# Expert layer of a graph network and feed-forward kernel: ten large and seven small steps in one slot space instead of thirteen and four, small ones placed between large ones, and the bias rows written one step later

## What is computed

```python
# x: (1250, 1024); _layernorm(x) is t
logits = silu(t @ rw1 + rb1) @ rw2 + rb2            # router, 8 experts
vals, idx = top_k(logits, 2)
w = softmax(masked to the two)                       # two weights per token
eh = silu(einsum('td,edh->teh', t, ew1) + eb1)       # 1024 -> 256, each expert
eo = einsum('teh,ehd->ted', eh, ew2) + eb2           # 256 -> 1024, each expert
y = t + einsum('te,ted->td', w, eo)
return x + y
```

## Time and profile before

| | us |
|---|---|
| median of 3 runs (1177.22 to 1178.97) | 1178.7 |
| the profiled execution, its own time | 1178.53 |
| its span, first to last instruction | 1176.7 |
| what lies around the span | 1.83 |
| first W1 matmul of step 0 | at 927.75 |
| first W1 matmul of step 1, of step 16 | at 943.29, at 1146.76 |

### The profile page before, as it was taken

One profiled execution on the slowest core, in us unless ns is written; L12 is line 12 of the kernel. 1 busy time (PEld: TensorE's weight loads), 2 busy tenths in 40 slices (PEclk: granted clock), 3 DMA queues, 4 the chain that ended last, 5 costly groups with the idle time before them and its releaser, 6 DMA issues.

```text
span 1176.7 us, 18108 instructions
## 1 busy us (share of the span) xinstructions
PE 1082.0 (92%) x6504; PEld 1025.6 (87%) x6504; DVE 630.8 (54%) x1115; ACT 446.1 (38%) x935; POOL 153.8 (13%) x171
## 2 busy tenths in 40 slices
PE   2699999999989999999999999999995599999984
PEld 1699999999989999999998999999994588898883
DVE  5738888888743353235333432642224467777762
ACT  5644444435311222121222021553332466666651
POOL 2000000000000001000100200014421223343311
PEclk9999999999999999999999999999997699999977
DMA  5402332123126560034003400765560779999973
GB/s 130 138 15 88 102 102 67 58 82 102 67 67 206 167 183 1 1 101 114 6 1 125 118 1 1 215 209 155 171 215 0 291 224 299 279 268 262 247 179 54
DMA packets 73658, 150.45 MB, mean 128 GB/s; under 512 B 12346, under 2 KB 51191, under 8 KB 69073
## 3 DMA queue, kind: packets, MB, share of 16 engines
q1 hardware_dynamic: 61117, 112.34, 30.8%
q0 software_dynamic: 11840, 36.22, 12.3%
q10 hardware_dynamic: 596, 0.48, 0.1%
HBM read 109.97 MB, written 44.53 MB: 131 GB/s over the span
## 4 chain that ended last, share of the span: by engine, by line
PE 76%; DVE 8%; DMA 5%; issue 5%; ACT 4%; DVEq 1%; ACTq 0%; POOL 0%; POOLq 0%; SPq 0%; PEld 0%
PE ps L1384 19%; PE ps L866 13%; PE ps L1456 9%; PE ps L1115 8%; PE ps L1423 7%; PE ps L2012 5%; DMA out<-o_rows,to_i 4%; PE ps L732 3%; PE ps L670 2%; PE ps L2028 2%; DVE w_lo L2094 2%; ACT w_hi L2048 1%; PE ps L654 1%; PE ps L1998 1%; DVE key_hot L725 1%
## 5 line engine op out<-in xcount | busy, mean ns | idle before, releaser
L739 DVE TENSOR_TENSOR adj<-ps,adj 125x250 f32 x212 | 87.8, 414 | 43.5 <-PE ps L732 35.4
L866 PE MATMUL ps<-h_lo,w_hi 128*128 128x418 f32 x336 | 108.5, 371 | 0.0
L1346 POOL TENSOR_TENSOR s_rows<-s_rows,b1t 125x1368 f32<-125x1368 f32 (+3 forms) x9 | 23.5, 2627 | 625.7 <-DMA s_rows<-in_x 625.7
L866 PE MATMUL ps<-h_hi,w_hi 128*128 128x418 f32 x336 | 100.3, 379 | 0.0
L1423 PE MATMUL ps<-z_hi,adj 125*125 125x342 f32 (+1 forms) x300 | 95.1, 322 | 1.6 <-DVE s_rows L1655 1.6
L1423 PE MATMUL ps<-z_lo,adj 125*125 125x342 f32 (+1 forms) x300 | 94.3, 319 | 1.9 <-issue 1.9
L866 PE MATMUL ps<-h_hi,w_lo 128*128 128x418 f32 x336 | 93.5, 359 | 0.0
L2012 PE MATMUL ps<-xt_hi,w_hi 128*128 128x256 f32 (+1 forms) x272 | 82.7, 304 | 10.1 <-DVE w_lo L2094 8.6
L1115 PE MATMUL ps<-adj,y_hi 125*128 125x416 f32 (+1 forms) x240 | 86.7, 361 | 3.4 <-issue 3.4
L2094 DVE TENSOR_TENSOR w_lo<-w_raw,w_hi 128x2048 fp32r<-128x2048 f32 x34 | 76.5, 2289 | 21.3 <-ACT w_hi L2048 19.9
L1115 PE MATMUL ps<-adj,y_lo 125*128 125x416 f32 (+1 forms) x240 | 86.2, 359 | 0.4 <-issue 0.4
(11 more groups left out here) (294 smaller groups left out, 2691.6 us busy)
## 6 DMA issues: line engine op xcount, KB each, us to landing
w_raw<-in_L_ffn_ew SPq DMA_DIRECT2D x34, 1024.0 KB
xin<-in_x SPq DMA_DIRECT2D x10, 448.0 KB
t_d<-xn SPq DMA_DIRECT2D x10, 448.0 KB
base<-x_d POOLq DMA_DIRECT2D x10, 448.0 KB, 4.1
out<-base POOLq DMA_DIRECT2D x10, 448.0 KB, 3.4
y_d<-y_hi SPq DMA_DIRECT2D x7, 625.0 KB
y_d<-y_lo SPq DMA_DIRECT2D x7, 625.0 KB
self_d<-self SPq DMA_DIRECT2D x7, 625.0 KB
```

The source lines that it names most:

```text
L739: e.tensor_tensor(cols, ps[0:P, 5 + b % 2, 0:KW].rearrange("p (t w) -> p t w", t=NT), cols, ALU.add).then_inc(self.took, 1)
L866: mm = e.matmul(BANK(m, own, c), wt[:, own, k, :], ht[:, k, a:a + w], start=(k == 0 and p == 0), stop=(k == KT - 1 and p == 2))
```

## The change

The table of slots gets 10 large and 7 small steps: still 17 steps, but 27 blocks (28 columns in the tables, which want an even count). Large steps own slots 0 to 2559 and small ones the 896 slots behind. A small remainder of an expert goes into a small step counted from the end, and into a large one from the end if the small ones are used up; the arithmetic for that replaces the old one by the same number of linked VectorE operations. A list `ORDER` says which step runs when. By size (L large, S small) the order of execution was L x13, S x4 and is now

`S L L S L S L L S L L S L S L L S`

On ScalarE `head(t)` now comes before `shift(t-1)`, and the wait for the slot weights and the bias rows moves from ahead of the first step into the first `shift`.

```diff
-BIG, SMALL = 13, 4
+BIG, SMALL = 10, 7
 NS = BIG + SMALL
-NBLK = BIG * SUB + SMALL
+BLOCKS_IN_USE = BIG * SUB + SMALL
+NBLK = BLOCKS_IN_USE + BLOCKS_IN_USE % 2
+ALL_SLOTS, BIG_SLOTS = 128 * BLOCKS_IN_USE, BIG * M
-BLOCKS = lambda s: SUB if s < BIG else 1
-BLOCK_AT = lambda s: min(SUB * s, BIG * (SUB - 1) + s)
+ORDER = (10, 0, 1, 11, 2, 12, 3, 4, 13, 5, 6, 14, 7, 15, 8, 9, 16)
+BLOCKS = lambda t: SUB if ORDER[t] < BIG else 1
+BLOCK_AT = lambda t: min(SUB * ORDER[t], BIG * (SUB - 1) + ORDER[t])
+BLOCKS_TO = lambda t: sum(BLOCKS(i) for i in range(t)) if t >= 0 else -SUB
...
-            link(e.tensor_scalar(at, at, first[:, 0, NX:NX + 1], None, ALU.add))
-            link(e.tensor_scalar(halved[:], at, 0.5, BIG * M / 2.0, ALU.mult, ALU.add))
-            link(e.tensor_tensor(jump[:], at, halved[:], ALU.min))
-            link(e.tensor_tensor(jump[:], jump[:], filled[:], ALU.subtract))
+            link(e.tensor_scalar(at, at, first[:, 1, NX:NX + 1], 2.0 * ALL_SLOTS, ALU.subtract, ALU.add))
+            link(e.tensor_scalar(halved[:], at, 0.5, None, ALU.mult))
+            link(e.scalar_tensor_tensor(out=at, in0=at, scalar=-float(BIG_SLOTS), in1=halved[:], op0=ALU.add, op1=ALU.min))
+            link(e.tensor_tensor(jump[:], at, filled[:], ALU.subtract))
             link(e.tensor_tensor(jump[:], jump[:], start, ALU.subtract))
...
                 for b in range(BLOCKS(s)):
                     for half in range(2):
-                        e.wait_ge(m_out, GROUP_AT(s - 1) + 2 * NB + 2 * b + half + 1)
+                        if s > 0:
+                            e.wait_ge(m_out, GROUP_AT(s - 1) + 2 * NB + min(2 * b + half + 1, 2 * BLOCKS(s - 1)))
...
             def shift(s, u, q):
-                x = e.value_load(step_x[0:1, ds(s, 1)], min_val=0, max_val=NX - 1)
+                x = e.value_load(step_x[0:1, ds(ORDER[s], 1)], min_val=0, max_val=NX - 1)
+                if s == 0:
+                    e.wait_ge(g_to, 2)
+                    e.wait_ge(g_b2, 16)
                 e.wait_ge(m_kept, s + 1)
...
             w1(0, 0, 0)
             rows(0, 0, 0)
-            e.wait_ge(g_to, 2)
-            e.wait_ge(g_b2, 16)
-            pipeline(e, NS, (1, shift), (0, head))
+            pipeline(e, NS, (0, head), (1, shift))
```

More of the change, by code:

```diff
@@ L63 @@
 SUB = M // 128
-BIG, SMALL = 13, 4
+BIG, SMALL = 10, 7
 NS = BIG + SMALL
-NBLK = BIG * SUB + SMALL
+BLOCKS_IN_USE = BIG * SUB + SMALL
+NBLK = BLOCKS_IN_USE + BLOCKS_IN_USE % 2
+ALL_SLOTS, BIG_SLOTS = 128 * BLOCKS_IN_USE, BIG * M
 for over_half in range(NX + 1):
     for under_half in range(NX - over_half + 1):
-        full = (TOP * N - (M // 2 + 1) * over_half - under_half) // M
-        assert full + over_half <= BIG and full + over_half + under_half <= NS
-BLOCKS = lambda s: SUB if s < BIG else 1
-BLOCK_AT = lambda s: min(SUB * s, BIG * (SUB - 1) + s)
+        bigs = (TOP * N - (M // 2 + 1) * over_half - under_half) // M + over_half
+        assert bigs + max(under_half - SMALL, 0) <= BIG or 2 * (bigs - BIG) + under_half <= SMALL
+ORDER = (10, 0, 1, 11, 2, 12, 3, 4, 13, 5, 6, 14, 7, 15, 8, 9, 16)
+assert sorted(ORDER) == list(range(NS))
+BLOCKS = lambda t: SUB if ORDER[t] < BIG else 1
+BLOCK_AT = lambda t: min(SUB * ORDER[t], BIG * (SUB - 1) + ORDER[t])
+BLOCKS_TO = lambda t: sum(BLOCKS(i) for i in range(t)) if t >= 0 else -SUB
 HK = HID // 128
@@ L1736, in _ @@
             e.iota(codei[:], [[-1, NX]], base=NX, channel_multiplier=0).then_inc(g_c, 1)
-            e.iota(stepi[:], [[M, NS]], base=0, channel_multiplier=0).then_inc(g_c, 1)
-            e.wait_ge(g_c, 8)
+            e.iota(stepi[:, 0:BIG], [[M, BIG]], base=0, channel_multiplier=0).then_inc(g_c, 1)
+            e.iota(stepi[:, BIG:NS], [[128, SMALL]], base=BIG_SLOTS, channel_multiplier=0).then_inc(g_c, 1)
+            e.wait_ge(g_c, 9)
             e.affine_select(out=belowm[:], in_=belowm[:], compare_op=ALU.is_gt, fill=0.0, base=0,
@@ L1748, in _ @@
             e.tensor_copy(stepm[:], stepi[:]).then_inc(g_c, 1)
-            e.wait_ge(g_c, 15)
+            e.wait_ge(g_c, 16)
             e.tensor_copy(before_b[:], before[:]).then_inc(g_c, 1)
@@ L1752, in _ @@
             for t in range(NT):
-                e.wait_ge(g_c, 17 + t)
+                e.wait_ge(g_c, 18 + t)
                 e.affine_select(out=same[:], in_=same[:], compare_op=ALU.not_equal, fill=1.0, base=-NX * t,
                                 pattern=[[-1, NX]], channel_multiplier=1).then_inc(g_c, 1)
-            e.wait_ge(g_c, 17 + NT)
+            e.wait_ge(g_c, 18 + NT)
             e.tensor_copy(same_b[:], same[:]).then_inc(g_c, 1)
@@ L1759, in _ @@
                             compare_op=ALU.is_gt, fill=0.0, base=0, pattern=[[NX, NT], [0, NX]], channel_multiplier=-1).then_inc(g_c, 1)
-            e.wait_ge(g_c, 19 + NT)
+            e.wait_ge(g_c, 20 + NT)
             e.tensor_copy(later_b[:], later[:].rearrange("p t n -> p (t n)")).then_inc(g_c, 1)
@@ L1770, in link @@
                 e.wait_ge(g_v, n[0])
-            e.wait_ge(g_c, 20 + NT)
+            e.wait_ge(g_c, 21 + NT)
             e.wait_ge(g_eb, 32)
@@ L1841, in _ @@
                                         scalar=-(NX + 1.0), in1=step_f[:], op0=ALU.mult, op1=ALU.add))
-            e.tensor_copy(step_x[:], step_f[:]).then_inc(g_x, 1)
+            e.tensor_scalar(step_x[:], step_f[:], 0.0, None, ALU.max).then_inc(g_x, 1)
             for c in range(TOP):
@@ L1919, in build @@
         NB = SUB * 2
-        GROUP_AT = lambda s: 2 * BLOCK_AT(s)
+        GROUP_AT = lambda s: 2 * BLOCKS_TO(s)
+        NTH = lambda s, b: 16 * sum(i % 2 == s % 2 and b < BLOCKS(i) for i in range(s + 1))
         WIDE = lambda s: 128 * BLOCKS(s)
@@ L1938, in head @@
             def head(s, u, q):
-                x = e.value_load(step_x[0:1, ds(s, 1)], min_val=0, max_val=NX - 1)
+                x = e.value_load(step_x[0:1, ds(ORDER[s], 1)], min_val=0, max_val=NX - 1)
                 for w, (raw, view) in enumerate(((w1_raw, w1_view), (w2_raw, w2_view))):
                     if s == 0 and w == 1:
-                        for b in range(SUB):
+                        for b in range(BLOCKS(0)):
                             e.wait_ge(m_xin[0][b], 16)
@@ L1959, in scatter @@
                     for b in range(BLOCKS(s - 1)):
-                        e.wait_ge(m_st[1 - u][b], 16 * (q + u))
+                        e.wait_ge(m_st[1 - u][b], NTH(s - 1, b))
                 e.sem_inc(m_kept, 1)
@@ L1992, in turn @@
                     for b in range(BLOCKS(s)):
-                        e.wait_ge(m_xin[u][b], 16 * q + 16)
+                        e.wait_ge(m_xin[u][b], NTH(s, b))
                 for g in groups:
@@ L2111, in tail @@
                 for b in range(BLOCKS(s)):
-                    e.wait_ge(m_eb, BLOCK_AT(s) + b + 1)
+                    e.wait_ge(m_eb, BLOCKS_TO(s) + b + 1)
                     for half in range(2):
@@ L2132, in _ @@
                 for b in range(SUB):
-                    e.wait_ge(m_st[u][b], 16 * sum(s % 2 == u and b < BLOCKS(s) for s in range(NS)))
+                    e.wait_ge(m_st[u][b], NTH(NS - 1 - (NS - 1 - u) % 2, b))
         with nc.Block() as block:
```

## The result

| | before | changed |
|---|---|---|
| median of 20 runs, us | 1178.55 | 1186.78 |
| lowest and highest | 1175.17, 1184.47 | 1175.66, 1195.29 |
| ratio, 95% interval | | 1.0047 [1.0024, 1.007] |

The changed kernel is slower, by 8.2 us between the medians and by 0.5% in the ratio (which leaves out the slowest two of the 20 runs). It also spreads over 20 us where the kernel before spreads over 9. The profile taken with the result is of an execution near the upper end, 1194.11 us; I profiled the kernel once more (`e10_after_again`) and got one near the lower end, 1173.11 us. The two are read side by side, since what is the same in both is the kernel and what differs is what the spread is made of.

What follows compares the result with a forecast made beforehand. A conversion chain nearly level with TensorE's transposes and W2 bounds the beat, ending last. Full clock -10.5, clock falls +14.4 and +4, end +2.5 make +10.4; 1176.7 becomes 1187.1 span, +1.83 is 1189 us; range 1171 to 1194.

Steps and rivals of the forecast that it cites:

- The chain sets the beat: From W1's end, SiLU and conversions through `w_lo` run 6.53 us; a W2 under about 6 us sets nothing, TensorE idles 2.7.
- Beats 2 to 15 at the full clock: Beats priced by step sizes sum to 176.78 us against 188.74 before, a difference of -12.0.
- late `xt_lo`: In small beats behind large ones, VectorE's `tail` and `xt_lo` can be late for the shorter W1: 1.5 us in all.
- The edit on ScalarE: SiLU is no longer queued behind a `shift` that waits for GpSimd: some 2.3 us in ten large beats.
- The clock: Six TensorE idles of 2.7 us after small W2s bring the granted clock down: +14.4 before small steps, +4 before large.
- Two such: +14.4: Clock falls after beats 4 and 12, before small steps, cost 7.2 us each; bounds 0 and 2 x 9.
- the sign named for beats 5 and 13: PEclk well under 1 in these two beats, which then last 18 to 20 us.
- The falls before a large step: After beats 1, 6, 9 and 14 a large W1 starts at the low clock: at most +1.5 each, +4 taken.
- The start: Step 0 ends its W1 about when it did and beat 1 has its 14.73 us again: no change.
- The end: Scatters are serial; step 15, now large, sends a second block 1.9 us later, and step 14 pushes it: +2.5 us.
- the clock holds: Rival: the short idles do not lower TensorE's clock, sum -8.0, 1170.5 us; chance 0.20.

Runs made afterwards that it cites:

- e10_after_again: The changed kernel run once more, unaltered, for a second profile: 1179.99 us median of 4 runs, ratio 1.0021.
- e2: The changed kernel with the next step's W1 converted right after the first half of the rows, on ScalarE and VectorE: 1147.67 us, ratio 0.9735.
- e1: The changed kernel with twelve unread matmuls put between the two halves of each small W2: 1171.01 us, ratio 0.9931.
- e3: The kernel before with only the ScalarE edit, head before shift, 13 large and 4 small steps kept: 1174.99 us, ratio 0.9963.
- e4: The changed kernel with its 10 large steps run first and the 7 small ones last: 1176.14 us, ratio 0.9981.
- e6: The kernel before, 13 large and 4 small steps, with the next step's W1 converted early and nothing else: 1167.28 us, ratio 0.9887.

## Why the prediction came out right

- **The chain sets the beat** (right). I took an idle time of 2.7 us after each of six small W2; it is 2.71 to 2.73. The evidence had been one gap of 0.40 instead of 0.22 us between two matmuls and one idle time of 2.37. e2 shows it from the other side: without the conversions on the chain the idle time is gone, and beat 4 falls from 12.28 to 9.39.
- **Beats 2 to 15 at the full clock** (right in the sum, in part by luck): 176.78 us from the rows, 176.66 in e1. Single kinds were off and cancelled: a beat with a small step between large ones was 12.63, not 12.40, the others were 0.1 to 0.2 shorter than I had them. The 1.5 us on top for late `xt_lo` did not come.
- **The edit on ScalarE** (right): I read 2.3 us from ten large beats; e3 has 2.6 there (135.14 - 132.50) and 3.8 in all.
- **The clock** (right mechanism, size off). The forecast was 14.4 + 4 = 18.4 us; by the medians of the changed kernel and e1 it is 15.8, by the ratios 13.7. In the first profile it is 193.83 - 176.66 = 17.2, in the second 181.41 - 176.66 = 4.8. The step "Two such: +14.4" priced every fall before a small step at 7.2 us, after one case that had lasted for most of its beat (0.59 in beat 15 before). It was 8.1 and 3.3 us in beats 13 and 5 of the first profile, and 1.6 in both of the second: how long the clock stays down varies. So the sign named for beats 5 and 13, "18 to 20 us", came true in none of the four cases: 20.72, 15.91, 14.28 and 14.27. The falls before a large step, +4 in the forecast, were 5.8 us in the first profile and 1.5 in the second.
- **The start** (off): I took 0. From the routing's first VectorE row to the first W1 of step 2 it was 59.18 before (898.84 to 958.02), and 61.0 and 59.4 in the two profiles of the changed kernel and 61.3 in e1: 0.2 to 2.1 us more.
- **The end** (right cause, size off): +2.5 forecast. From the first W1 of step 16 it was 29.94 before; it is 33.8 to 34.4 now, 3.9 or more. The last scatters of the second execution:

```profile
1151.52 1.56 POOL L1971 DMA_INDIRECT out<-o_rows,to_i  x1 [6.29 <-DVE o_rows L2125]
1153.38 1.56 POOL L1971 DMA_INDIRECT out<-o_rows,to_i  x1 [0.30 <-issue]
...
1161.11 1.56 POOL L1971 DMA_INDIRECT out<-o_rows,to_i  x1 [6.17 <-DMA out<-o_rows,to_i]
```

The second block of step 15 goes out 1.86 us after the first, and step 16 waits 6.17 us for it where it waited 5.33 in the earlier trace rows: two blocks also take longer to land than one. The rest, 1.1 us, is step 14, whose two scatters push 15. The first row names VectorE, whose two parts of the block had been ready since 1149.60; before, that scatter came 0.8 us behind such a part, now 1.9, as it also waits for step 14's second block, which went out at 1143.67 and took 7.0 us to land.

The rival "the clock holds" is e1: 1170.5 forecast, 1171.01 measured. With the start and the end together 2 to 3 us dearer, and the clock 3 and the late `xt_lo` 1.5 cheaper, 1189 became 1186.8. The mechanism is shown by e1, e2 and e4. That the number agrees within 2 us is luck as well: the same program gave single times from 1173 to 1195, and the four later runs have a median of 1179.99.

## What to carry to other kernels

When two engines' chains are nearly level, price a shorter piece of work by what ends last beside it: three steps cut in half were worth nothing here (e4 against e3), and the whole change 14 to 20 us once the chain was cut as well (e2 against e6, with or without the edit on ScalarE). Look for the small gap between matmuls even where a window says 99% busy (133.54 of 135.14 us). Idle time that costs nothing in itself can cost the clock; matmuls that fill it may be the cheapest repair, and moving the wait is the better one.

## What the hardware showed that I had not expected

- A W1 half of 24 float32r matmuls takes 2.63 us with 128 columns and 2.98 with 256: half the columns, 12% less time. At 1.2 GHz, 5.16 with 128 columns.
- After an idle time of 2.4 to 2.7 us the granted clock fell to 1.2 GHz in some executions and not in others of the same program: before beat 10 of the changed kernel 2.7 us brought it to a mean of 0.88 in the first profile and left it at 1.00 in the second. What decides it is open. It fell most dearly where a small W1 followed: 16.60, 17.05, 20.25 (behind 3.7 us) and 20.72 us for beats that take 11.5 to 12.6 at 2.4 GHz. But two such beats took only 14.3.
- Up to 6.3 us of difference between two executions of one program arose ahead of the part that was changed.
